# A Mamba-2 block and a ternary feed-forward on one core: a re-staged first tile, with one convolution block and the decay operands moved to GpSimd

## What is computed

```
xn = x * rsqrt(mean(x*x) + eps)
z, xbc, dt_raw = split(xn @ w_in)            # 512, 768, 8 columns
xc = silu(causal_conv4(xbc) + conv_b)        # 4 taps for each of 768 channels
dt = softplus(dt_raw + dt_bias); a = -exp(a_log) * dt
y  = chunked_scan(xc, dt, a) + d_skip * xh   # decays are exp of sums of a
h  = x + (rmsnorm(y * silu(z)) * norm_w) @ w_out
x  = layernorm(x + h + relu(rmsnorm(h) @ w_fc)**2 @ w_proj)
x  = layernorm(x + ffn(x))                   # w1, w2, h1, h2, w3: ternary, in float32
```

## Time and profile before

| | us |
|---|---|
| runs | 1303.56, 1303.59, 1298.61 (median 1303.56) |
| profiled execution, its own time | 1302.72 |
| its span, first to last instruction | 1300.7 |
| TensorE matmuls busy | 1208.8 (93%) |
| VectorE busy | 794.3 (61%) |
| ScalarE busy | 644.7 (50%) |
| GpSimd busy | 257.9 (20%) |

### The profile page before, as it was taken

The page is one execution under the profiler, slowest core; times in us unless marked ns, Lnnn a source line. Parts: engine busy times, 40 slices in busy tenths (PEclk is TensorE's granted clock), DMA queues, the critical chain, the costliest instruction groups (busy, mean ns, idle before and its releaser), DMA issues.

```text
span 1300.7 us, 19143 instructions
## 1 busy us (share of the span) xinstructions
PE 1208.8 (93%) x6450; PEld 1013.7 (78%) x6450; DVE 794.3 (61%) x1385; ACT 644.7 (50%) x1231; POOL 257.9 (20%) x221
## 2 busy tenths in 40 slices
PE   3559999999999999998699999999999999999996
PEld 2347787888888888876588888888888888888885
DVE  2759788898989898974433633536335363353633
ACT  3627888788878787865321413224133241332410
POOL 0621625353534434351000000000000000000000
PEclk9769999999999999999799999999999999999998
DMA  6021312131212213122520000100001000010000
GB/s 211 1 75 61 86 61 86 57 96 37 90 67 87 75 59 102 38 84 87 235 120 1 17 17 1 32 0 13 19 0 32 0 9 23 0 32 0 8 9 18
DMA packets 30440, 66.54 MB, mean 51 GB/s; under 512 B 4032, under 2 KB 22080, under 8 KB 28736
## 3 DMA queue, kind: packets, MB, share of 16 engines
q1 hardware_dynamic: 30400, 66.01, 15.1%
HBM read 57.59 MB, written 19.94 MB: 60 GB/s over the span
## 4 chain that ended last, share of the span: by engine, by line
issue 51%; POOL 0%; DVE 0%; POOLq 0%; DVEq 0%
POOL rsv_b L1695 0%; DVE o_sb L1771 0%; POOLq L1693 0%; DVEq L1529 0%; POOLq L359 0%
## 5 line engine op out<-in xcount | busy, mean ns | idle before, releaser
L1681 ACT ACTIVATE full<-bank,scale 128x512 f32<-128x512 f32 x128 | 88.3, 690 | 383.9 <-PE bank L1584 383.9
L1584 PE MATMUL bank<-hB_lo,h_sb 128*128 128x512 f32 x512 | 200.2, 391 | 0.0
L1584 PE MATMUL bank<-hB_hi,h_sb 128*128 128x512 f32 x512 | 199.7, 390 | 0.0
L1584 PE MATMUL bank<-hA_hi,h_sb 128*128 128x512 f32 x512 | 199.2, 389 | 0.0
L1584 PE MATMUL bank<-hA_lo,h_sb 128*128 128x512 f32 x512 | 199.2, 389 | 0.0
L1746 DVE CAST hA_hi<-full 128x512 fp32r<-128x512 f32 x64 | 27.3, 427 | 185.9 <-ACT full L1681 185.9
L1695 POOL TENSOR_TENSOR rsv_b<-mv_b,eps 128x4 f32<-128x4 f32 x8 | 10.7, 1341 | 655.2 <-DVE mv_b L186 655.2
L1162 DVE SCALAR_TENSOR_TENSOR xc<-xp,conv_w_sb,xc 128x512 f32<-128x512 f32 x144 | 113.9, 828 | 5.2 <-ACT xc L762 5.1
L1584 PEld LDWEIGHTS bank<-hA_lo,h_sb 128*128 128x128 f32 x512 | 96.1, 188 | 20.0
L1584 PEld LDWEIGHTS bank<-hA_hi,h_sb 128*128 128x128 f32 x512 | 96.1, 188 | 20.1
L1584 PEld LDWEIGHTS bank<-hB_hi,h_sb 128*128 128x128 f32 x512 | 96.2, 188 | 19.2
(11 more groups left out here) (205 smaller groups left out, 3024.3 us busy)
## 6 DMA issues: line engine op xcount, KB each, us to landing
chk_xh<-w_ffn SPq DMA_DIRECT2D x16, 704.0 KB, 4.3
ffn_raw<-w_ffn SPq DMA_DIRECT2D x8, 1408.0 KB, 7.9
h_sb<-ffn_raw SPq DMA_DIRECT2D x2, 4096.0 KB, 17.6
x_in<-x SPq DMA_DIRECT2D x8, 512.0 KB, 4.7
xT<-x_t SPq DMA_DIRECT2D x8, 512.0 KB, 4.6
x_res<-x SPq DMA_DIRECT2D x8, 512.0 KB, 3.9
x_rows<-x SPq DMA_DIRECT2D x8, 512.0 KB, 3.4
x_in<-x_rows SPq DMA_DIRECT2D x8, 512.0 KB, 4.4
```

Source lines behind the costliest of these rows:

```text
L1584: ins = pe.matmul(o, a_, b_, start=first and n == 0, stop=last and n == 1, skip_group_check=True)
L1681: nc.scalar.activation(full[:, n % FULL, :], b[:], ACT.Gelu, scale=scale[:, 1 + n // KH, n % KH:n % KH + 1]).then_inc(s_gd, 1)
```

## The change

The scan, the loops of both phases and every loop instruction stay. In the head and in iteration 0:

- tile 0's x comes in two halves, each with its own semaphore, in chunk order; w_in comes in two transfers, its columns for xBC and dt ahead of `xT` and its z columns behind the small parameters;
- the row `x_rstd` isn't made for tile 0. VectorE scales the columns of the identity by `rsx` (4 instructions into `y`), and one float32 matmul of a matrix of ones with it puts the row on all partitions of a PSUM bank. VectorE multiplies `xT` by it in two halves, and hi and lo parts follow by halves;
- both parts of w_in's low half are made by GpSimd;
- w_fc and w_proj are copied within memory to `mlp_raw` (the layout of SBUF), and loaded from there into `hT` and `m`, which are now tiles that hold both parts; `E` and `chk_xh` are no longer staging places. `load_half(0, 0)` and `copy_piece(0)` stand ahead of `spread_rstd(1)`, and the wait for all low parts is gone from SyncE;
- the hi and lo parts of w_out, w_fc and w_proj are made in iteration 0 (`split_hi` on ScalarE, `split_lo` on GpSimd);
- VectorE does dt and a ahead of the taps, and five of the six convolution blocks; block 1 is done by GpSimd (`head_taps`, six instructions), with `decay_operands` behind it; `sums(0)` stands after the third block instead of after z;
- silu of convolution blocks and of z alternate on ScalarE.

```diff
                 sp.sem_inc(s_x1o, 1)
-                load_x(0, 0)
+                for n, sm_ in enumerate((s_xh0, s_x)):
+                    part = rows(x, 0)[:, 2 * n:2 * n + 2, :]
+                    sp.dma_start(x_in[:, 2 * n:2 * n + 2, :], part).then_inc(sm_, 16)
+                w_in_rows = w_in.rearrange("(k p) n -> p k n", p=P)
+                sp.dma_start(w_in_st[:, :, XBC], w_in_rows[:, :, XBC]).then_inc(s_stage[0], 16)
                 load_xT(0, 0)
...
+                sp.dma_start(w_in_st[:, :, Z], w_in_rows[:, :, Z]).then_inc(s_wz, 16)
...
+                sp.wait_ge(s_mraw, 32)
+                for n in (2, 3):
+                    sp.dma_start(staged[n][0], mlp_raw[n - 2]).then_inc(s_stage[n], 16)
+                load_half(0, 0)
                 load_residual(0, 0)
                 load_x(1, TILE * D)
                 load_xT(1, TILE)
+                copy_piece(0)
                 spread_rstd(1)
-                sp.wait_ge(s_wlo, len(staged))
-                load_half(0, 0)
-                copy_piece(0)
...
+                pe.wait_ge(s_diag, CH)
+                pe.matmul(pj_banks[0][:], ones[:], y[:].rearrange("p b n -> p (b n)")[:, 0:TILE], start=True,
+                          stop=True).then_inc(s_rs0, 1)
                 pe.wait_ge(s_wdt, 2)
+                pe.wait_ge(s_xnl0, 1)
                 dt_rows(w, 0)
+                pe.wait_ge(s_wlx, 1)
+                for m in CONV_ORDER[:3]:
+                    xbc(w, 0, m)
+                sums(0)
+                for m in CONV_ORDER[3:]:
+                    xbc(w, 0, m)
                 pe.wait_ge(s_wlo, 1)
...
+                def head_taps(m):
+                    pool.wait_ge(s_ad, w_head.act(f"xbc{m}") + 1 + ACT_BANKS)
+                    for n in range(TAPS - 1):
+                        part = u[:, n % 2, :]
+                        nc.gpsimd.tensor_tensor(part, xp[:, m, n:n + TILE],
+                                                conv_w_sb[:, m, n:n + 1].broadcast_to([P, TILE]), ALU.mult).then_inc(s_ptap, 1)
+                        pool.wait_ge(s_ptap, 2 * n + 1)
+                        ins = nc.gpsimd.tensor_tensor(xc[:, m, :], xc[:, m, :], part, ALU.add)
...
+                def split_lo(n):
+                    st, hi, lo, _ = staged[n]
+                    pool.wait_ge(s_whi, n + 1)
+                    nc.gpsimd.tensor_tensor(flat3(lo), st, flat3(hi).bitcast(F32), ALU.subtract).then_inc(s_wlo, 1)
```

Where `split_lo` stands in GpSimd's iteration 0:

```diff
                     make_ud(w, i, 1)
+                    if not mlp:
+                        split_lo(1)
                     decay_state(i, 1)
...
                     make_ud(w, i, 2)
+                    if not mlp:
+                        split_lo(2)
                     decay_state(i, 2)
...
                     make_ud(w, i, 3)
+                    if not mlp:
+                        split_lo(3)
                     decay_state(i, 3)
```

More of the change, by code:

```diff
@@ L286, in post_ln_block @@
                   (x1[:].rearrange("p c n -> p (c n)"), w_out_hi, w_out_lo, w_out),
-                  (E[:].rearrange("p b h n -> p (b h n)"), w_fc_hi, w_fc_lo, w_fc),
-                  (chk_xh[:, 0:KH * D], w_pj_hi, w_pj_lo, w_proj)]
+                  (hT[:].rearrange("p b k n -> p (b k n)").bitcast(F32), w_fc_hi, w_fc_lo, w_fc),
+                  (m[:].rearrange("p b j n -> p (b j n)")[:, 0:KH * D].bitcast(F32), w_pj_hi, w_pj_lo, w_proj)]
+        w_in_st = staged[0][0].rearrange("p (k n) -> p k n", k=KD)
+        XBC, Z = slice(INNER, PROJ), slice(0, INNER)
         flat3 = lambda ap: ap[:].rearrange("p k n -> p (k n)")
@@ new lines, in _ @@
+                sp.dma_start(w_in_st[:, :, Z], w_in_rows[:, :, Z]).then_inc(s_wz, 16)
+                dst, hi, lo, src = staged[1]
+                sp.dma_start(dst.rearrange("p (k n) -> p k n", n=D), src.rearrange("(k p) n -> p k n", p=P)).then_inc(s_stage[1], 16)
+                for n in (2, 3):
+                    src = staged[n][3]
+                    part = mlp_raw[n - 2].rearrange("p (k n) -> p k n", n=src.shape[1])
+                    sp.dma_start(part, src.rearrange("(k p) n -> p k n", p=P)).then_inc(s_mraw, 16)
@@ L740, in hi_part, with x_rms @@
                     nc.scalar.activation(dst, banks[w.dve_bank(name)][:], ACT.Copy).then_inc(s_hi, 1)
-                def x_rms(step, t):
-                    act.wait_ge(s_x, 16 * t + 16)
+                def x_rms(step, t, halves=False):
+                    act.wait_ge(s_xh0 if halves else s_x, 16 * t + 16)
                     for c in range(CH):
+                        if halves and c == CH // 2:
+                            act.wait_ge(s_x, 16)
                         step.link(nc.scalar.activation(junk[:, 0:D], x_in[:, c, :], ACT.Square,
@@ L956, in _ @@
                 act.wait_ge(s_masks, MASKS)
-                x_rms(step, 0)
+                x_rms(step, 0, halves=True)
                 act.wait_ge(s_stage[0], 16)
[L959 to L963, removed]
+                nc.scalar.activation(w_dt[:, :, 0:HEADS], w_in_st[:, :, PROJ - HEADS:], ACT.Copy).then_inc(s_wdt, 1)
@@ L976, in _ @@
-                for c in range(CH):
-                    z_silu(w, 0, c)
-                for n in range(MC):
-                    conv_silu(0, n)
-                sums_hi(0)
-                act.wait_ge(s_wlo, len(staged))
+                act.wait_ge(s_wz, 16)
+                nc.scalar.activation(w_in_hi[:, :, Z], w_in_st[:, :, Z], ACT.Copy).then_inc(s_whi, 1)
+                w = w_head
+                act.wait_ge(s_wlo, 1)
+                softplus(step, w)
+                for m in CONV_ORDER[:3]:
+                    xbc(w, 0, m)
@@ new lines, in _ @@
+                sums_hi(0)
+                for m in CONV_ORDER[3:]:
+                    xbc(w, 0, m)
+                head_silu = lambda ready, n, m: (act.wait_ge(ready, n), nc.scalar.activation(
+                    xc[:, m, :], xc[:, m, :], ACT.Silu, bias=conv_b_sb[:, m:m + 1]).then_inc(s_xc, 1))
+                head_silu(s_cv, 2, 4)
+                head_silu(s_cv, 3, 0)
+                z_silu(w, 0, 0)
+                head_silu(s_cv, 4, 2)
+                z_silu(w, 0, 1)
+                head_silu(s_cvp, 1, 1)
@@ L982, in _ @@
+                z_silu(w, 0, 2)
+                head_silu(s_cv, 5, 3)
+                z_silu(w, 0, 3)
+                head_silu(s_cv, 6, 5)
                 assert step.n == X_STEPS + DT_STEPS
```

171 lines of the change are left out of this document (99 added, 72 removed).

## The result

The changed kernel took 1280.52 us (median of 4 runs, 1278.17 to 1281.81), against 1301.85 for the kernel before on the same chip (4 runs): a ratio of 0.984, with an interval from 0.981 to 0.986. The forecast was 1279, a gain of 23.8; the medians differ by 21.3. The profiled execution had 1278.17, with a span of 1276.5 against 1300.7.

A forecast was written before the change was run, and what follows sets the result against it. Head and iteration 0 were taken to bound the change: late normalized x, taps held by GpSimd, the half-piece wait. -28.0 (shorter head, no wait) + 6.2 (splits) - 2.0 (clock) = -23.8, so 1279 us, range 1269 to 1290.

The forecast's parts named there:

- The first matmul: Head, TensorE: first `dt_rows` matmul at 13.8 us instead of 21.23, -7.4; as a sign, 12.5 to 16.
- The spread: Head: the reciprocal root, spread by scaled identity and a float32 matmul, is in PSUM at 10.0 us.
- The taps: Head, VectorE: last convolution tap ends at 41.2 us instead of 54.44.
- From the last tap to `y_diag`: Head into iteration 0: from 41.2 us, first mask exponents at 44.0, `y_diag` of chunk 0 at 50.2.
- The half piece: Iteration 0: its wait goes, `y_diag` of chunk 0 at 50.2 us instead of 78.20, -28.0 with the head's -16.2 included.
- The splits' price: Iteration 0: three weight splits moved there give back 6.2 us (nothing, 1.7 and 4.5), between 3 and 12.4.
- The clock: Iteration 0: TensorE may stay at full clock without the 13 us pause, -2.0 us (0 to 3.5).
- the full clock by 60: Sign in iteration 0: TensorE near full clock by 60 us.
- the missing wait: Sign in iteration 0: no wait for the half piece.
- the held instructions: Sign in iteration 0: VectorE instructions of 4 to 5 us beside `w_fc_lo` and `w_pj_lo`.
- the full lock: Rival: SBUF port lock costs all 12.4 us in iteration 0, no clock help; -15.6, 1287 us; chance 0.19.
- The late half piece: Rival: half piece delayed behind SyncE's `mlp_raw` wait; break-even landing 68.5 us, 1310 us if at 76; chance 0.03.

The follow-up runs named there:

- the repeat: The changed kernel measured once more with no edit, beside the kernel before: 1283.2 us, ratio 0.986 (0.984 to 0.988).
- the run with two edits: Changed kernel with all six convolution blocks on VectorE and both w_in splits behind xn's low part: 1276.47 us, ratio 0.981 to the kernel before.

## Why the prediction was right

The gain was forecast at 23.8 us and is 21.3 by the medians. The absolute numbers, 1279 and 1280.5, lie closer, since the kernel before measured 1301.85 beside the changed one and not 1303.56. The mechanisms were those forecast: no wait for the half piece, a shorter head, splits that hold VectorE in iteration 0. Several of the parts were off, and some of them cancelled:

- **The first matmul, -7.4 forecast, -3.3 measured.** This is the largest error of the forecast. It had GpSimd's xBC split hold up the first half of `xnT_lo`, and then let both halves through; the z split, which it placed at 13.3 to 15.9 itself, was only asked when `xp` would be free. It held the second half to 17.2. The run with both splits behind xn's low part puts `dt_rows` at 13.56, where the forecast had 13.8 for another reason. w_in's landing was off as well: 60% of the words landed at 9.22, not 7.2. The spread was fine, 9.6 for 10.0; but VectorE then stood until `xT` had landed, 10.5.
- **The taps.** Forecast from 21.35 to 41.2, 19.85 long; measured from 25.47 to 45.56, 20.1 long. The length was right, the parts less so: the scaling of w_out was not in the sum with a price, and took 4.23 instead of 1.13 beside `head_taps`; the taps lost less. No row of before had shown these four scalings beside GpSimd. That this block on GpSimd is a loss in itself was right: without it the last tap is 2.4 earlier.
- **From the last tap to `y_diag`.** Forecast 9.0, measured 7.2. The forecast had taken this stretch from before, where it ran at the low level; now the first exponents took 0.70 for 1.19 and `y_off` 1.02 for 1.52, with a granted clock of 0.91 and 1.00 in the windows 45 to 50 and 50 to 55. That is 1.0 of the 1.8; the rest is not traced.
- **The half piece.** No wait, as forecast. Added alone to the kernel before, it brings 14.7 of 18.3 us by the medians and 11.5 of 20.9 by the projection; taken out of the changed kernel, it costs 14.9 (16.8 by the projection). It is the largest part of the change. `y_diag` was at 52.8 for 50.2, -25.4 for -28.0.
- **The splits' price, +6.2 forecast, 7.2 to 8.6 measured** by leaving w_fc's and w_proj's out (3.0 and 4.3 at once, or 3.6 and 3.6 against the repeat; forecast 1.7 and 4.5). By the times it is 3 to 6. w_fc's split held the scores of chunk 2, and behind it the decay product of `S` (73.45 to 75.47 on GpSimd) held one small `dt` instruction (74.50, 1.02 for some 0.2) and the skip product the next (75.55, 0.97). w_out's split, priced at nothing, was taken out in no run. Of the forecast's 4.9 us for ScalarE's copies, its own rate makes 4.6 for the 5120 words; it took them as covered, so nothing hangs on it. The Trainium skill, page "SBUF — State Buffer", section "SBUF: two separate sides", names the instructions of VectorE that take the shared pair, one "in a 2-port perf mode, or with two SBUF inputs". The 32-column `sm` of L1269 and the scaling of w_out have one input from SBUF, and were held, so the trace agrees, if these run in such a mode. Their pace speaks for it: `chk_xh<-chk_xh` with 704 words takes 0.53 and the scaling of 256 words 0.28, 0.56 ns for each word more, while a `TENSOR_TENSOR` takes 0.68 for 512 and 1.21 for 1024, 1.04 ns for each. The forecast had used only the part on two inputs.
- **The clock, -2.0 forecast.** `y_diag` of chunk 0 took 1.97 for 3.65, which is 1.7. It didn't stay up: it was 0.50 again from 60 to 62, where `y_diag` of chunk 1 took 2.67, and 0.66 from 90 to 100. Without the two splits `y_diag` to projection takes 53.0 us, against 55.5 before; that difference of 2.5 also holds whatever else differs in the stretch, and no run parts the clock's share from the rest. What is given back in all is 6.0, or 4.8 in the repeat; forecast was 4.2.
- **Together:** 4.1 late at the first matmul, 0.2 in the taps, 1.8 won behind them and 1.8 more given back make -19.4 at iteration 1's projection, where the forecast had -23.8. Behind it more came: 1.6 in the profiled repeat (22.4 in own time, 20.8 at that projection), 4.8 in the profiled first run. About 2 appear by iteration 2 in both; no experiment was made on what makes them, and it stays open. So some 2 us of the gain come from a term that the forecast didn't have; that they offset half of its shortfall is luck.

Of its signs, the first matmul (12.5 to 16), the last tap (near 41) and the full clock by 60 didn't come; `y_diag` (47 to 54), the missing wait and the held instructions did. Of the rivals, that of the full lock had 12.4 us for the three splits; two of them cost 7.2 to 8.6, more than the forecast had for all. But its other condition, no help from the clock, fell: `y_diag` ran in 1.97. The late half piece didn't come either: SyncE's wait for `mlp_raw` ended at 19.1, and the piece was there at 28.6, far from 68.5.

## What to carry to other kernels

Before an edit to a tuned head is priced, ask which single transfer or wait ends last behind it: here the issue of one transfer carried more than half of the gain. Then look at what the edit moves behind the part that it shortens: with that transfer late, a head 13 us shorter brought `y_diag` 12 us forward, and the work moved into iteration 0 was part of the 8 us that it then gave back. When work of GpSimd is moved, list every VectorE instruction with its operands in SBUF, small ones too, that falls under each stretch of it, at the new place as at the old, since the price moved with the work in each of the runs that moved it. And a VectorE gain ahead of a lull of TensorE is to be read together with the granted clock behind the lull.

## What the runs showed of the hardware

- A gain of 2 us on VectorE vanished in TensorE's clock. With the taps over 2.4 us sooner, the granted clock was 0.50 from 44 to 50, and the exponents and `y_off` ran at 1.2 GHz; it fell again from 53 under `y_diag` (2.82 for 1.97); in the unedited kernel work of lesser weight (z's last block, 42.4 to 45) ran under the low level in their stead. No run changed VectorE's pace and kept z's last block where it was, so that the clock took the gain is read from the windows. With w_out's scaling moved, `y_diag` took 3.16.
- Fewer bytes didn't land sooner: w_in's first part of 776 KB took 7.3 us from issue to landing, as the 1288 KB of before did. Both had x's transfers ahead of them; between 3.9 and 5.0 us the changed kernel's DMA moved 119 to 145 GB/s, after 371 to 378 in the 1.1 us ahead of it (199 after 334 in the repeat). Why it sagged there was not tried, and the landing varies: in the run with two edits it took 5.3.
- A scaling of 128x256 words by a column of 128 took 0.28 alone and up to 1.6 on average beside GpSimd's instructions (for four: 1.13 alone; 3.57, 4.23, 5.79 and 6.25). Even the 8 words a partition of `neg_a` took 1.95 beside the z split in the version with two edits, for 0.16 in the changed kernel.
